# Masked attention of a 16-part network on one core: whole score matmuls, a separate matmul for the later keys, and maxima moved to the query stack without DRAM

## The reference

```python
def _L2_attn_b_ref(hidden_states, Wq, bq, Wk, bk, Wv, bv, Wo, bo):
    ...
    scores = jnp.einsum('bihd,bjhd->bhij', q, k) / scale
    blk = jnp.arange(S) // WINDOW          # WINDOW = 32
    allowed = blk[:, None] >= blk[None, :]
    scores = jnp.where(allowed, scores, jnp.zeros((), scores.dtype))
    probs = jax.nn.softmax(scores, axis=-1)
    ctx = jnp.einsum('bhij,bjhd->bihd', probs, v).reshape(B, S, H)
    return ctx @ Wo.T + bo
```

## Time and profile before

| | us |
|---|---|
| median of 3 runs | 4212.86 (4212.06 to 4240.83) |
| profiled execution, whole | 4234.49 |
| profiled execution, span | 4233.2 |
| PE busy | 3652.4 (86%) |
| DVE busy | 2555.6 (60%) |
| ACT busy | 2279.3 (54%) |
| POOL busy | 1198.6 (28%) |

### The profile page before, as it was taken

One profiled execution on the slowest core, in us unless ns is written; L12 is line 12 of the kernel. 1 busy time (PEld: TensorE's weight loads), 2 busy tenths in 40 slices (PEclk: granted clock), 3 DMA queues, 4 the chain that ended last, 5 costly groups with the idle time before them and its releaser, 6 DMA issues. The chain is left out here.

```text
span 4233.2 us, 49302 instructions
## 1 busy us (share of the span) xinstructions
PE 3652.4 (86%) x17104; PEld 1736.7 (41%) x17104; DVE 2555.6 (60%) x6048; ACT 2279.3 (54%) x5022; POOL 1198.6 (28%) x1004
## 2 busy tenths in 40 slices
PE   4769999899988888988888886789979999888987
PEld 1324444443344454434444442334423344454334
DVE  5896433434587767666777689983444334655564
ACT  4556663536546566646656666562344522465663
POOL 3463232321234544103455355540000000000320
PEclk8899999999989899979989898899977899787875
DMA  3000000000000001110000010000221000402320
GB/s 131 0 0 1 1 1 1 0 1 0 0 1 1 1 1 54 51 40 13 1 1 1 1 50 0 0 1 0 55 68 37 23 1 25 111 20 42 82 43 11
DMA packets 82706, 92.14 MB, mean 22 GB/s; under 512 B 26056, under 2 KB 71816, under 8 KB 80408
## 3 DMA queue, kind: packets, MB, share of 16 engines
q1 hardware_dynamic: 82456, 88.98, 7.7%
HBM read 62.11 MB, written 26.02 MB: 21 GB/s over the span
## 5 line engine op out<-in xcount | busy, mean ns | idle before, releaser
L332 ACT ACTIVATE scratch<-psum 128x512 f32<-128x512 f32 (+10 forms) x1988 | 957.6, 505 | 1276.5 <-PE psum L304 1116.1
L343 POOL TENSOR_TENSOR scratch<-scratch 128x512 f32<-128x512 f32 (+3 forms) x536 | 690.8, 1296 | 1523.7 <-ACT scratch L332 1216.0
L304 PE MATMUL psum<-scratch,w_experts 128*128 128x512 f32 (+3 forms) x2192 | 1037.9, 608 | 29.5 <-ACT scratch L332 22.0
L304 PE MATMUL psum<-scratch 128*32 128x256 f32 (+16 forms) x6432 | 705.3, 347 | 113.7 <-ACT scratch L332 31.2
L343 DVE TENSOR_TENSOR scratch<-scratch,psum 128x512 f32<-128x512 f32 (+2 forms) x732 | 462.2, 636 | 444.1 <-PE psum L304 432.5
L332 ACT ACTIVATE scratch<-scratch 128x255 f32<-128x255 f32 (+9 forms) x1264 | 549.8, 463 | 158.9 <-DVE scratch L347 53.3
L304 PEld LDWEIGHTS psum<-scratch,w_experts 128*128 128x128 f32 (+3 forms) x2192 | 393.1, 188 | 530.7 <-issue 435.0
L304 PEld LDWEIGHTS psum<-scratch 128*32 128x32 f32 (+8 forms) x6432 | 362.9, 136 | 464.3 <-issue 244.9
L304 PE MATMUL psum<-scratch,w_constants 128*128 128x512 f32 (+2 forms) x848 | 458.0, 635 | 24.7 <-ACT scratch L332 14.3
L355 DVE TENSOR_TENSOR_SCAN scratch<-scratch 128x512 f32<-128x512 f32 x256 | 364.6, 1425 | 73.9 <-POOL scratch L343 73.7
L304 PE MATMUL psum<-scratch,w_early 128*128 128x512 f32 (+11 forms) x912 | 318.9, 493 | 62.0 <-DVE scratch L343 28.2
(11 more groups left out here) (97 smaller groups left out, 3692.6 us busy)
## 6 DMA issues: line engine op xcount, KB each, us to landing
q_stack<-scratch SPq DMA_DIRECT2D x72, 192.0 KB, 2.8
scratch<-q_out SPq DMA_DIRECT2D x96, 96.0 KB
q_out<-scratch SPq DMA_DIRECT2D x40, 192.0 KB, 3.0
scratch<-q_stack SPq DMA_DIRECT2D x24, 288.0 KB
w_local<-q_stack SPq DMA_DIRECT2D x16, 288.0 KB
scratch<-q_out SPq DMA_DIRECT2D x24, 192.0 KB
w_experts<-q_out SPq DMA_DIRECT2D x24, 192.0 KB
w_experts<-L_experts_dram SPq DMA_DIRECT2D x1, 4356.0 KB, 12.9
```

The costliest lines, as they stand in the source:

```text
L304: return self.engine.matmul(out, lhsT, rhs, start=start, stop=stop, **kw)
L332: return self.engine.activation(out, src, function, **kw)
L343: return self.engine.tensor_tensor(out, a, b, op)
```

## The change

In the masked part alone:

- `pe_scores` makes whole scores with two matmuls of 83 x 128 by 256 queries, as the unmasked part does. The scores of later keys get NEG in them (the 8 block rows are in both stacks), so their exponential is 0. `only_maxima` and the 8 small matmuls are gone.
- What later keys contribute, exp(-max) times the sum of their values, is computed apart, once a unit: `pe_turn_maxima` now transposes minus the maximum repeated 16 times (`many`, 128 columns), so that 128 rows come out; `act_max` takes the exponential of rows 64 to 127 (`zero_exp`, 64 x 256); `dve_max` multiplies it by `own_block`; two matmuls with the constant `later` sum the values of later keys (64 x 72); `dve_max` spreads these sums into `later_sums`. Each `pe_values` (two a unit) starts with one f32 matmul, 64 rows of contraction, 128 x 256 out, that puts this share into the bank; the eight matmuls of before add to it.
- New waits: `pe_scores` of step 0 waits for `later sums_out`, `pe_values` for `later exp_masked`, the first exponential of maxima for the previous unit's `pv`, the turn of the sums for `later exp`.

In all three attentions: `sp_maxima` sends each of the three parts of the maxima with its own DMA from SBUF to its row of `q_rows`; the DMA to DRAM, the wait for it and the DMA back are gone. `act_max` of the next unit waits for the arrival instead of for the sending. `v_wide` is 9 columns shorter, SCRATCH goes from 6212 to 6400 columns.

```diff
     def pe_scores(self, e, u, i):
-        q, k, n, a = self.q_rows[u % 2], self.k_rows[u % 2], self.STACK, v2(self.a, TOKENS)
+        q, k, a = self.q_rows[u % 2], self.k_rows[u % 2], v2(self.a, TOKENS)
...
-        if not self.masked:
-            for c in range(2):
-                last = e.matmul(a[:, c, :], k[:, i, c * P:(c + 1) * P], q[:, i, :])
-        else:
-            e.matmul(a, self.m["only_maxima"][0:self.rows], over(q[:, i:i + 1, :], [self.rows, 2, TOKENS]), stop=False, skip_group_check=True)
-            for c in range(2):
-                for r in range(4):
-                    first = c * P + 32 * r
-                    last = e.matmul(a[32 * r:32 * r + 32, c, first:], k[0:n, i, first:first + 32], q[0:n, i, first:], start=False,
-                                    skip_group_check=True)
+        elif self.masked:
+            e.wait_ge(*(yield self["later", "sums_out", u]))
+        for c in range(2):
+            last = e.matmul(a[:, c, :], k[:, i, c * P:(c + 1) * P], q[:, i, :])
...
     def pe_turn_maxima(self, e, u, before):
...
+            if self.masked:
+                last = e.transpose(self.half_b[:, cols], self.many[:, t].rearrange("p b h -> p (b h)"), self.c["ident"])
...
+        if self.masked:
+            for c in range(2):
+                at = ((u // 2 * 2 + c) * HEADS8 + u % 2 * self.HALF) * (HD8 + 1)
+                last = e.matmul(self.a[P // 2:, 0:self.HALF * (HD8 + 1)], self.w["later"][:, c * P // 2:(c + 1) * P // 2],
+                                self.v_wide[:, at:at + self.HALF * (HD8 + 1)], start=(c == 0), stop=(c == 1))
+            last.then_inc(*self.post("later", "sums", u))
...
     def pe_values(self, e, u, s):
...
+        if self.masked:
+            e.wait_ge(*(yield self["later", "exp_masked", u]))
+            e.matmul(self.b[:, 0:TOKENS], self.later_sums[:, s * P:(s + 1) * P], self.zero_exp, skip_group_check=True)
...
     def act_max(self, e, u):
...
-            e.wait_ge(*(yield self["maxes", (u - 1) % 2, u - 1, "sent"]))
+            e.wait_ge(*(yield self["maxes", (u - 1) % 2, u - 1]))
...
+        if self.masked:
+            if u:
+                e.wait_ge(*(yield self["pv", u - 1, 1]))
+            e.activation(self.zero_exp, self.half_b[P // 2:], ACT.Exp, scale=HD8 ** -0.5).then_inc(*self.post("later", "exp", u))
...
     def dve_max(self, e, u):
...
+            e.tensor_tensor(self.many, over(self.minus_max.unsqueeze(2), shape), over(self.c["minus_floor"].unsqueeze(2).unsqueeze(3), shape),
+                            ALU.min).then_inc(*self.post("maxima", "minus_max", u))
...
+            e.tensor_tensor(out, here, over(self.w["own_head"][P // 2:].unsqueeze(2), [P // 2, self.HALF, n]), ALU.mult).then_inc(*self.post("later", "sums_out", u))
+            e.wait_ge(*(yield self["later", "exp", u]))
+            e.tensor_tensor(self.zero_exp, self.zero_exp, self.m["own_block"][P // 2:], ALU.mult).then_inc(*self.post("later", "exp_masked", u))
...
     def sp_maxima(self, e):
...
-            e.dma_start(self.s.max_out[slot].rearrange("i h n -> h i n"), self.max_parts).then_inc(*self.post_dma("maxes", slot, u, "sent"))
-            e.wait_ge(*(yield self["maxes", slot, u, "sent"]))
             e.wait_ge(*(yield self["stack", slot, u]))
-            e.dma_start(self.q_rows[slot][m], self.s.max_out[slot]).then_inc(*self.post_dma("maxes", slot, u))
+            for i in range(3):
+                row = self.max_row + i
+                e.wait_ge(*(yield self["maxima", "max_parts", u, i]))
+                e.dma_start(self.q_rows[slot][row:row + 1], self.max_parts[:, i, :]).then_inc(
+                    *self.post_dma("maxes", slot, *((u,) if i == 2 else (u, "part", i))))
```

More of the change, by code:

```diff
@@ L109, in masks @@
     out["row_ones"] = np.ones((3, TOKENS))
-    out["only_maxima"] = np.tile(np.arange(83)[:, None] >= 80, (1, P)).astype(float)
+    out["own_block"] = (k // 32 == q % 64 // 8).astype(float)
     out["block_of_query"] = (k // 32 == blocks).astype(float)
@@ L202, in layouts @@
                     **{w: as_cols(by_channel(p[n + w][None])) for w in ("bq", "bk")}, "bo": as_cols(p[n + "bo"]),
-                    "bv": as_rows(p[n + "bv"])}
+                    "bv": as_rows(p[n + "bv"]),
+                    "later": np.concatenate([(np.arange(P)[:, None] + c * P) // 32 > np.arange(64)[None] // 8 for c in range(2)], 1).astype(np.float32),
+                    "own_head": (np.arange(P)[:, None] % 8 == np.arange(8)[None]).astype(np.float32)}
     n = "L2_ffn_"
@@ L249 @@
 PATIENCE = 500
-SCRATCH = 6212
+SCRATCH = 6400
 class Engine:
@@ L1313, in lay_out @@
         self.max_rest = self.xn[0:H, TOKENS:2 * TOKENS]
-        self.max_parts = self.take_bf16(3 * TOKENS, parts=H).rearrange("p (i n) -> p i n", n=TOKENS)
+        if self.masked:
+            self.many = self.take(2, P).rearrange("p t (b h) -> p t b h", h=H)
+        small = self.take(3 * TOKENS // 2)
+        self.max_parts = small[0:H].bitcast(BF16).rearrange("p (i n) -> p i n", n=TOKENS)
+        self.zero_exp, self.later_sums = small[P // 2:, 0:TOKENS], self.xn[P // 2:, TOKENS:2 * TOKENS]
         mark = self.used
@@ L1420, in pe_values @@
                 last = e.matmul(self.b[32 * j:32 * j + 32, 0:TOKENS], self.v_wide[:, at:at + 32],
-                                self.pt[j][:, c * TOKENS:(c + 1) * TOKENS], start=(c == 0), skip_group_check=True)
+                                self.pt[j][:, c * TOKENS:(c + 1) * TOKENS], start=(c == 0 and not self.masked), skip_group_check=True)
         last.then_inc(*self.post("pv", u, s))
@@ L1521, in dve_start @@
                         self.a.rearrange("p (t h c) -> p t h c", h=HEADS8, c=HD8), ALU.add).then_inc(*self.post("token", "v_tok"))
+        if self.masked:
+            e.memset(self.later_sums, 0.0).then_inc(*self.post("later", "zeroed"))
     def dve_maximum(self, e, u, i):
@@ L1530, in dve_max @@
         e.wait_ge(*(yield self["maxima", "max", u, self.STEPS - 1]))
-        floor = over((self.c["minus_floor"] if self.masked else self.c["no_floor"]).unsqueeze(2), [P, 2, self.HALF])
-        e.tensor_tensor(self.minus_max, self.minus_max, floor, ALU.min).then_inc(*self.post("maxima", "minus_max", u))
+        if self.masked:
+            shape = [P, 2, 16, self.HALF]
+            e.tensor_tensor(self.many, over(self.minus_max.unsqueeze(2), shape), over(self.c["minus_floor"].unsqueeze(2).unsqueeze(3), shape),
+                            ALU.min).then_inc(*self.post("maxima", "minus_max", u))
+        else:
+            floor = over(self.c["no_floor"].unsqueeze(2), [P, 2, self.HALF])
+            e.tensor_tensor(self.minus_max, self.minus_max, floor, ALU.min).then_inc(*self.post("maxima", "minus_max", u))
         e.wait_ge(*(yield self["maxima", "max_parts", u, 0]))
```

21 lines of the change are left out of this document (15 added, 6 removed).

## The result

The changed kernel takes 4170.49 us (median of 4 runs, 4153.66 to 4172.43) against 4221.64 us for the kernel before beside it: a ratio of 0.9864 [0.9817, 0.9912]. So it is 1.4% to 1.8% faster, 51 to 82 us by the medians; 56 were forecast. Its profiled execution took 4172.43 us, span 4171.1, with a mean granted clock of 0.908 (before 0.894).

What follows compares the result with a forecast made beforehand. PE was taken as the bound (86% busy), with attention alone also costing gaps and a low clock; -58 + 31 - 42 - 12 + 15 + 15 - 5 = -56 us from 4212.9 gave 4157 us, range 4092 to 4240.

Steps and rivals of the forecast that it cites:

- Term 4: On ACT, 135 more table loads of 1.283 us, mostly covered by idle ACT: +15 us, between 0 and 65.
- Term 5: At the program's end, more of stream 3's work runs in low-clock chains of single streams: +15 us, bounds 0 and 25.
- Term 6: The rest: ending the maxima's DRAM detour saves 11 us, more issues and later buffer release cost 5: -5 us rounded.
- Term 1: In masked attention, two score matmuls replace nine, saving 0.48 us a step alone and 0.35 beside experts: -58 us.
- Term 2: In masked attention, added f32 matmuls for the later keys' share and sums, time proportional to columns: +31 us.
- Term 3: The planner's new order puts more attention and `L3_blocks` steps beside experts: -42 us from mixing, -12 from a closed gap.
- the gap: PE's wait of 16 us when the second stream pair enters masked attention together; expected to go, worth 12 us.
- The formula: Pricing of steps moved beside experts, masked attention 25 us and `L3_blocks` 38: 63 for perfect mixing, two thirds taken, 42.
- Only the arithmetic counts: Rival, 27%: mixing gives nothing, table loads delay the moved steps and the end repays the skew; 4190 to 4205 us.
- ACT becomes the bound: Rival, 13%: in mixed attention, expert and `L3_blocks` stretches, exposed table loads make the kernel slower, 4250 to 4278 us.
- Its variant: Each table switch holds the activation behind it 2.57 us, so 51 exposed loads give 4278 us; 2 of the 13%.
- The scheduling luck: Reordering of the parts from `L1_attn` to `L2_scan`: +/- 15 us in every case, no case of its own.

Runs made afterwards that it cites:

- e10: The changed kernel in its own order, each masked score step issued as the old nine matmuls, planner charged for two: 4193.43 us, 0.9905.
- e12: The changed kernel itself run again later, beside other kernels on the same chip: 4154.66 us, 0.9818 of the kernel before.
- e9: The changed kernel in its own order without the 32 f32 matmuls for the later keys' share, planner still charged: 4119.30 us, 0.9729.
- e4: The kernel before, same instructions, reordered by raising the planner's semaphore price from 90 to 120 ns: 4165.49 us, 0.9858.
- e11: The changed kernel planned with a semaphore price of 125 ns: 4162.09 us, 0.9832.
- e6: The changed kernel planned with a semaphore price of 120 ns: 4150.42 us, 0.9786.
- e2: The kernel before with only the direct DMAs of the maxima from SBUF, old arithmetic: 4181.79 us, 0.9896.
- e7: The kernel before, same instructions, planned with a semaphore price of 100 ns: 4244.78 us, 1.0018.
- e5: The changed kernel in its own order, SiLUs of both `L2_experts` issued as copies, so 152 of 408 table loads go: 4148.61 us, 0.9788.
- e8: The changed kernel planned with a semaphore price of 100 ns: 4284.15 us, 1.0103.

## Why the prediction was right, step by step

The sum was right, 56 us against 51 to 82, but by luck: its terms made each other good. The arithmetic brought some 27 us less than forecast, the order and the rest some 22 us more, or still more by the second comparison. Term 4 held within what could be measured, Term 5 was not settled, and of Term 6 nothing is seen.

**Term 1, score matmuls (-58): the mechanism right, mis-sized.** The durations were right to 0.03 us. But in the new order (e10 against e12) a step brings 0.29 us, not 0.45: 37 us (25 to 50) for 128. A small part is the mix of levels: the sum put 56% of 102 steps at the low level, where 33 of all 128 start in e10 (47 in the kernel before), which makes 52 of the 58. The profiled executions differ by 48, the means by 37; whether the rest is scatter of the executions or work that does not reach the end is open. Terms 1 and 3 shared a gain: a step that is moved into full clock no longer saves its low-level price. By the packing rule of the Trainium skill ("TensorE: Matmul & The Clock Gate", "Part 3: Packing small matmuls — row/col tiling") Term 1 would have been 48, nearer to what was measured; but not for the rule's reason, for the eight small matmuls still take 0.43 us at the low level in e10, the prediction's 0.44.

**Term 2, added matmuls (+31, 24 of it for the share): mis-sized.** The share costs 37 us (28 to 47, e9 against e12). Its own time in e12's trace is the forecast's 24 us, but by two errors that cancelled. "Time proportional to columns" was too low: 0.62 and 1.15 us instead of 0.48 and 0.97. And 56% at the low level was too much: 7 of the 32 are wholly in it. Of the 0.62 us, 0.53 are those of such a matmul anywhere; the rest stands ahead of the matmuls on column strips, and no run separates it. What the term left out is the clock, which is higher when the share is gone. The sums, some 7 us in the prediction, were not measured alone. Together the arithmetic of the change nets -37 + 37, give or take 19, and the sums: about nothing, where -27 had been forecast. Each half was priced with the other in place; the old arithmetic whole in the new order was not run.

**Term 3, the new order (-54): right in kind, and worth more.** Measured 51 to 82, less an arithmetic of about 0, leaves the order and the rest at -51 to -82 where Terms 3 to 6 said -29. This is a remainder and carries the arithmetic's 19 us. e4 shows it without any of the change: -1.42%, 60 us. Two of its signs came as named: the gap went (16.2 to 1.0 us), the clock rose to 0.908. The third came nearly: the stretch with a clock near 0.7 shrank from 200 us to about 100 (0.71 from 3123 to 3223 us). But the gap is not what counts: in e4 PE waits for the stacks' DMAs as long as before (7.5 + 13.8 us against 16.2 + 3.4). Nor is the count of mixed steps a measure of it: 61/11 (e4), 76/30 (after) and 105/31 (e11) differ by no more than 0.5 points, 72/25 (e6) is the best of all, 49/15 (e2) gives 1.0%, 24/1 (e7) nothing. The formula priced the attentions alone; the last part, with 16 us after the change and 12 in e4, is not in it. Nor did the clock rise in the stretch of `L3_blocks` (0.79, then 0.77), for which it had 25 of its 42 us. The order's worth was found by running; the formula only had its sign and rough size.

**Term 4, table loads (+15): within what was measured.** 0.08 to 0.21 us a load make 11 to 28 us for 135, if they cost what the 152 of e5 cost; against e12 alone nothing is not excluded. ACT was 170.5 us busier (180 named), PE's waits for it went from 148.7 to 125.5 us, and DVE's grew by 30.

**Term 5, the end (+15): not settled.** The emptier end came as named: in the last 150 us PE is busy 109 us at a clock of 0.56, before 122 at 0.64. Yet stream 3's last part took 57 us instead of 73, with fewer others beside it (84 instructions of PE in it, before 172). No run prices the one against the other.

**Term 6, the DMAs (-5): not seen.** PE waits as long for the direct DMAs as for the detour (10.6 against 9.0 us). The three DMAs of one row each are slow to issue on SP. After, in the first attention, and before, the same step:

```profile
1710.69 2.22 SPq L406 DMA_DIRECT2D w_experts<-scratch  x3
1719.26 0.64 SPq L406 DMA_DIRECT2D scratch<-scratch  x1
```

```profile
1716.45 0.27 SPq L404 DMA_DIRECT2D max_out<-scratch  x1
1717.86 0.23 SPq L404 DMA_DIRECT2D w_experts<-max_out  x1
```

2.22 us pass from the first issue to the end of the last, where before it was 1.64, the wait for the first one's landing included.

**The rivals.** *Only the arithmetic counts* fell twice: the arithmetic counts for about nothing net, and an order alone brings as much as the change (e4). *ACT becomes the bound* fell with e5: not 50 loads are exposed but the worth of 25 at most. Its variant, a load that holds its activation for twice its row, fell with it; the Trainium skill's drain ("ScalarE: Activation LUTs", "What ACT_TABLE_LOAD costs") is seen neither in the 0.02 us behind a load nor in e5's price. The rival that ends slower was real, but by another way than the one written: e8 has the whole change and 238 loads, fewer than the kernel before, and is 1% slower. Its order hardly mixes, but that of e7 does not either and costs nothing, so the cause is open. The scheduling luck, put at 15 us, is more like 30 (the spread of the pairs).

What stays open: why e8 loses 54 us or more outside the masked part against e7, and what in an order makes it fast. The runs show that the order carries the gain; how much of it is the mixing, how much the streams' distance at the end and how much the luck of an order, they do not show.

## What to carry to other kernels

Where a planner makes the order, any edit is two: its own and a new order. Price them apart, the edit in a frozen order (charge the planner for the old instructions, emit the new ones) and the order by a planner constant on the old kernel, before a gain is booked to the edit. A matmul's saving is to be taken at the clock of the place where it will stand, not of the place where it stood, and its level read instruction by instruction, not from a stretch's mean. And a stretch cut at one stream's starts says how that stream fares; before a gain in it is put down to a part, count the instructions in it.

## What the runs showed of the hardware

- A DMA of 4 KB from SBUF into one row of SBUF takes SP 0.63 us to issue (median of the 144 of the changed kernel, 0.62 to 0.72); those of 12 KB to and from DRAM take 0.27 and 0.23 (48 each before).
- An f32 matmul of 64 rows, 128x256 out, ahead of eight on column strips takes 0.62 us at the high level and 1.15 at the low one; one of the same shape ahead of another takes 0.53, and half of a 128x512 one is 0.48.
- In one order, nine small matmuls a step instead of two brought the granted clock of a stretch from 0.87 to 0.76, and leaving 32 f32 matmuls out brought it to 0.91, with PE busy 181, 188 and 178 of 200 us; one execution each, and the first kernel had 0.85 in another one.
